# Root of the variance in the first node stage: ACT's square root for two blocks in place of a Newton iteration on DVE

## The chip, the cores and the metric

The kernel runs on one core of a Trainium2 chip. The metric is the device time of one execution in microseconds (us): the median of 3 runs was 4217.27 us before the change (4213.93 to 4219.17).

## What is computed

A graph network of four layers over 50,000 nodes with 160 features and 25,000 edges. Every layer ends with a layer norm. Cut to layer 0:

```python
x = layernorm(x + L0(x, node_vec1, edge_attr_4, edge_attr_8, weights, src, dst))   # and so for L1, L2, L3

def layernorm(x, eps=1e-05):
    m = mean(x, axis=-1); v = var(x, axis=-1)
    return (x - m) / sqrt(v + eps)

# L0, after the edges' messages are summed per node into agg and mapped to ms, conv:
sc    = linear(x) * node_attr
angle = 0.1 * (ms @ W3) * node_attr / sqrt(96)
return cos(angle) * sc + sin(angle) * conv
```

Features are held as 64 scalars and 3 x 32 vector components.

## The kernel before

The kernel goes through the layers one by one, each in two stages. An **edge stage** gathers the rows of source nodes, computes messages and writes sums per node to the tensor `aggregates`. A **node stage** goes over the nodes and writes the layer's output. The node stage works on 100 blocks (NBLK) of 512 nodes: 128 partitions with four nodes each, so a block is a tile of 128 x 640 (`xn`, `an`, both in `arena`), held in a ring of 8 (NRING). Every engine has its own instruction sequence, and the order of work is written out by hand: `steps` calls an engine's function for every block b (some 12 blocks unrolled, the rest in a loop of 8 bodies), and waits on semaphores tie the engines together. "Body b" below is one call of such a function. Engines run at different distances from one another, since each body also handles earlier blocks.

In layer 0 the node stage does this:

- **SP** loads x and aggregates (L470, L459).
- **PE** (`node_products`), body b: transposes block b (L794), then the products of block b-1 with the self weights, eight matmuls (L816) that fill one PSUM bank for nodes 0 to 2, and four (L820, L821) that fill the second. `sc_ready` counts both banks.
- **ACT** (`node_copies`), body b: issues the store of block b-5 (L926), copies the transposed block b out of PSUM to `nT` (L930), normalizes block b-4 by four instructions with `rstd` as scale and `shift` as bias (L950), and in even bodies computes Abs and two sines for the pair of blocks that begins at b+2 (`sines`, L909, L910, L912).
- **POOL** (`node_moves`): in even bodies the gates of a pair from its sines (L596, L597), a copy of gate inputs (L563), and the angles of the next pair, a chain of eight small steps (L578 to L585) that ends with `trig_ready`. In every body it multiplies the aggregates by a gate (L625) and adds them to x (L632), which counts `x_added`.
- **DVE** (`node_vectors`), body b: four multiply-adds that add the gated products to x (L1268; the first two wait for the first bank of products and for `x_added`, the third for the second bank), four `bn_stats` (L1276), four `bn_aggr` (L1287) that leave mean and variance in `mv` and count `mv_ready`. In even bodies the root of the variance of the pair (b-2, b-1) is interleaved with these: `root()` issues the next instruction of a chain of twelve. It adds EPS (L1204), makes a guess from the bits as an int32 operation (L1205), does three Newton steps (L1207, L1208, L1209), which end in `rstd`, and computes `shift` = -mean x rstd (L1210). Each waits for the one before by `root_chain`, and `shift_ready` lets ACT normalize.

Layers 1 to 3 have no such chain: ACT computes `std` by Sqrt per block (L944), DVE the reciprocal and the shift (L1233, L1238). Where ACT's next function isn't in the table that is loaded, the compiler puts an ACT_TABLE_LOAD into the sequence. Before the change layer 0 has none between Silu of its edge stage and Sin, Abs, Copy and Identity of its node stage, and layers 1 to 3 have one each ahead of their first Sqrt.

Of the kernel before, what the change touches and what calls it, by code (L numbers as in the profile page):

```python
# [22 lines left out]
P = 128  # L23
BT = 4
NBLK = 100
# [25 lines left out]
ZN = 3240  # L51
TWO_PI_HI = 6.28125
TWO_PI_LO = float(2 * np.pi - 6.28125)
GUESS = float(0x5f3759df)
ROUND = 12582912.0

r = lambda n: float(1.0 / np.sqrt(float(n)))
# [87 lines left out]
def steps(eng, first, last, steady, body, ring=RING):  # L145

    lo, hi = steady
    for q in range(first, lo):
        body(q, q % ring, q // ring)
    with eng.Fori(0, (hi - lo) // ring) as i:  # L150
        for k in range(ring):
            body(i * ring + (lo + k), k, i + lo // ring)
    for q in range(hi, last):
        body(q, q % ring, q // ring)


def within(q, lo, hi):

    return lo <= q < hi if isinstance(q, int) else True
# [14 lines left out]
def build(nc, nodes, front, back_rows, gate_rows, pairs, eattr, main, small, self_rows, out):  # L174
# [3 lines left out]
    with ctx:  # L178
        def sb(name, shape, dt=f32):
            return ctx.enter_context(nc.sbuf_tensor(name, shape, dt))  # L180

        def sem(name):
            return ctx.enter_context(nc.semaphore(name))
# [54 lines left out]
        stats = sb("stats", [P, 2, BT, 6])  # L238
        mv = sb("mv", [P, NRING, BT, 2])
        std = sb("std", [P, NRING, BT])  # L240
        var = sb("var", [P, 2, BT])
        newton = sb("newton", [P, 3, 2, BT])
        rstd = sb("rstd", [P, NRING, BT])
        shift = sb("shift", [P, NRING, BT])
        gates = sb("gates", [P, NRING, BT, 2])
# [72 lines left out]
        tot_ready, carried, tot_out = sems("tot_ready", 2), sems("carried", 2), sem("tot_out")  # L318


        y_part, count_max = sem("y_part"), sem("count_max")
        TRIG_OPS, ROOT_OPS = 8, 11
        PC2 = TRIG_OPS // 2 * NBLK
        x_in, a_in, stored = sems("x_in", NRING), sems("a_in", NRING), sems("stored", NRING)
        nturned, nturned_out, sc_ready = sem("nturned"), sem("nturned_out"), sem("sc_ready")
# [522 lines left out]
        def _(act):  # L848
# [8 lines left out]
            for l in range(4):  # L857
# [60 lines left out]
                def node_copies(b, k, turn):  # L918
                    if within(b, STORE_LAG[l], NBLK + STORE_LAG[l]):
                        kk, tt = back(k, turn, STORE_LAG[l], NRING)  # L920
                        done = b - STORE_LAG[l]
                        if not isinstance(b, int):
                            done = act.snap(done)
                        act.wait_ge(normed, node_count(l, b - STORE_LAG[l]))
                        alone(act, passed["act"])
                        act.dma_start(orows[bass.ds(done, 1)].rearrange("o p c -> (o p) c"), xn[:, kk]).then_inc(stored[kk], 16)  # L926
                    if within(b, 0, NBLK):
                        act.wait_ge(nturned, node_count(l, b))
                        wait(act, sc_ready, 2 * (b + (l * NBLK - 1)))
                        nc.scalar.activation(nT[:, k % 2, :], two_banks[k % 2][:, 0:5 * P], ACT.Copy).then_inc(nturned_out, 1)  # L930
                        if l == 0 and isinstance(b, int) and b == 0:
                            sines(b, k)
                    if l == 3 and within(b, 0, NBLK):
                        act.wait_ge(gates_ready, b + (2 * NBLK + 1))
                        act.wait_ge(a_in[k], node_slot(l, k, turn) * 16)
                        alone(act, passed["act"])
                        for j in range(BT):
                            row = an3[:, k, j, F:2 * F]
                            last = nc.scalar.activation(row, row, ACT.Copy, scale=gates[:, k, j, 1:2])  # L939
                        last.then_inc(second_gated, 1)  # L940
                    if l and within(b, SQRT_LAG, NBLK + SQRT_LAG):
                        kk, tt = back(k, turn, SQRT_LAG, NRING)
                        act.wait_ge(mv_ready, node_count(l, b - SQRT_LAG))
                        nc.scalar.activation(std[:, kk, :], mv[:, kk, :, 1], ACT.Sqrt, bias=eps[:, :]).then_inc(std_ready, 1)  # L944
                    if within(b, APPLY_LAG[l], NBLK + APPLY_LAG[l]):
                        kk, tt = back(k, turn, APPLY_LAG[l], NRING)
                        act.wait_ge(shift_ready, node_count(l, b - APPLY_LAG[l]))
                        for t in range(BT):
                            row = xn[:, kk, t * F:(t + 1) * F]
                            last = nc.scalar.activation(row, row, ACT.Identity,  # L950
                                                        bias=shift[:, kk, t:t + 1], scale=rstd[:, kk, t:t + 1])
                        last.then_inc(normed, 1)
                    if l == 0 and k % 2 == 0 and within(b, 0, NBLK - 2):
                        sines(b + 2, (k + 2) % NRING)
# [5 lines left out]
        def _(dve):  # L960
# [135 lines left out]
            for l in range(4):  # L1096
# [98 lines left out]
                def node_vectors(b, k, turn):  # L1195
                    k2 = k % 2
                    base = b * 2 + 2 * l * NBLK
                    kk, tt = back(k, turn, 1, NRING)
                    ka = (k - 2) % NRING if k % 2 == 0 else 0
                    stt = nc.vector.scalar_tensor_tensor  # L1200

                    v, (y, a, c) = var[:, :, :], (newton[:, n] for n in range(3))
                    R = rstd[:, ka:ka + 2, :]
                    ops = [lambda: nc.vector.tensor_scalar(v, mv[:, ka:ka + 2, :, 1], EPS, None, ALU.add),  # L1204
                           lambda: nc.vector.tensor_scalar(y.bitcast(i32), v.bitcast(i32), -0.5, GUESS, ALU.mult, ALU.add)]  # L1205
                    for n in range(3):
                        ops += [lambda: stt(out=a, in0=y, scalar=-0.5, in1=v, op0=ALU.mult, op1=ALU.mult),  # L1207
                                lambda: nc.vector.tensor_tensor(c, a, y, ALU.mult),  # L1208
                                lambda to=y if n < 2 else R: stt(out=to, in0=c, scalar=1.5, in1=y, op0=ALU.add, op1=ALU.mult)]  # L1209
                    ops.append(lambda: stt(out=shift[:, ka:ka + 2, :], in0=mv[:, ka:ka + 2, :, 0], scalar=-1.0, in1=R,  # L1210
                                           op0=ALU.mult, op1=ALU.mult))
                    done = [0]
                    rooted = l == 0 and k % 2 == 0 and within(b, 2, NBLK + 1)

                    def root(n=1):
                        for _ in range(n):
                            i = done[0]
                            if not rooted or i > ROOT_OPS:
                                return
                            if i == 0:  # L1220
                                dve.wait_ge(mv_ready, b)
                            else:
                                dve.wait_ge(root_chain, (b - 2) * ROOT_OPS + 2 * i)
                            if i < ROOT_OPS:
                                ops[i]().then_inc(root_chain, 2)
                            else:
                                ops[i]().then_inc(shift_ready, 2)
                            done[0] += 1
# [60 lines left out]
                            last.then_inc(mv_ready, 1)  # L1289
                        root()  # L1290

                steps(dve, 0, NBLK + 1, NODE_STEADY, node_vectors, NRING)

# [36 lines left out]
```

## Time and profile before

| what | value |
|---|---|
| median of 3 runs | 4217.27 us (4213.93 to 4219.17) |
| profiled execution: its own time | 4216.08 us |
| its span, first to last instruction | 4214.4 us |
| busy share of the span | PE 85%, DVE 70%, POOL 61%, ACT 52% |
| node stage of layer 0 | about 700 to 1210 us |
| mean granted TensorE clock, whole span | 0.935 of full speed |

Busy shares of the whole span are averages over eight stages that differ in what limits them. The profile is one execution; the time outside its span is 1.7 us. In its views a line number is one of the kernel before, a name `arena<-bank` says what an instruction writes and reads, "x4" counts merged instructions, and a part in brackets gives the idle time ahead of it and what ended it.

### The profile page before, as it was taken

How to read it: one execution, taken by the hardware profiler on the slowest of the kernel's cores; microseconds unless marked ns; L12 is line 12 of the kernel's file. 1: busy time of each engine (PE TensorE's matmuls, PEld its weight loads, DVE VectorE, ACT ScalarE, POOL GpSimd, SP SyncE). 2: the span in 40 equal slices, each digit the busy share in tenths (PEclk: the TensorE clock that was granted, in tenths of full speed). 3: DMA queues.
4: the chain of work that ended last, by engine and by line, in shares of the span. 5: the costliest groups of instructions: out<-in, count | busy, mean ns of one | idle time of the engine just before them, and what ended most of it. 6: DMA issues, size and time to landing. Idle time of an engine off the chain costs nothing. (4 is left out here: it accounts for less than half of the span.)

```text
span 4214.4 us, 104663 instructions
## 1 busy us (share of the span) xinstructions
PE 3591.9 (85%) x27044; PEld 3337.9 (79%) x27044; DVE 2936.2 (70%) x10747; ACT 2187.2 (52%) x5797; POOL 2567.6 (61%) x3126
## 2 busy tenths in 40 slices
PE   0699997666669999899989999899799999877676
PEld 0599996656569999877779999777699999866566
DVE  0577775888866666488856666688766666588888
ACT  0244443555544444377744444577655555477777
POOL 0377776777757777500057777444456666488887
PEclk9999998777779999999989999999999999988988
DMA  9522223666556555488832222588622222277775
GB/s 380 183 74 62 60 54 99 197 200 201 198 164 178 174 173 171 140 284 299 294 81 62 61 58 52 172 281 280 225 69 74 73 69 62 62 260 259 246 257 193
DMA packets 469538, 682.78 MB, mean 162 GB/s; under 512 B 212838, under 2 KB 285502, under 8 KB 465672
## 3 DMA queue, kind: packets, MB, share of 16 engines
q1 hardware_dynamic: 333546, 389.79, 30.2%
q0 software_dynamic: 75376, 125.21, 10.6%
q10 hardware_dynamic: 60512, 166.57, 10.0%
q8 instruction: 44, 0.72, 0.1%
q14 instruction: 60, 0.49, 0.0%
HBM read 391.37 MB, written 314.78 MB: 168 GB/s over the span
## 5 line engine op out<-in xcount | busy, mean ns | idle before, releaser
L537 POOL DMA_INDIRECT aggregates<-arena,meta x784 | 793.3, 1012 | 445.0 <-issue 240.8
L950 ACT ACTIVATE arena<-arena,shift,rstd 128x160 f32<-128x160 f32 x1600 | 697.2, 507 | 180.2 <-DVE shift L1210 177.7
L717 PE MATMUL bank<-same_all,msg 128*98 (+1 forms) x6272 | 753.4, 274 | 0.0
L528 POOL DMA_INDIRECT xg<-x_after,meta x588 | 575.9, 979 | 272.1 <-issue 251.0
L717 PEld LDWEIGHTS bank<-same_all,msg 128*98 128x98 f32 x6272 | 711.1, 166 | 0.0
L884 ACT ACTIVATE w<-bank 1x162 f32<-1x162 f32 (+1 forms) x784 | 257.2, 328 | 788.1 <-PE bank L750 782.2
L750 PE MATMUL bank<-w,arena 98*128 98x32 f32 (+1 forms) x4704 | 626.3, 270 | 0.0
L816 PEld LDWEIGHTS bank<-sc_cols,nT 128*128 128x128 f32 x2400 | 360.4, 221 | 290.2 <-issue 288.9
L750 PEld LDWEIGHTS bank<-w,arena 98*128 98x128 f32 x4704 | 588.0, 192 | 0.0
L1268 DVE SCALAR_TENSOR_TENSOR arena<-bank,attr,arena 128x160 f32<-128x160 f32 x1600 | 519.9, 378 | 88.3 <-PE bank L816 25.4
L816 PE MATMUL bank<-sc_cols,nT 128*128 128x128 f32 (+1 forms) x2400 | 373.0, 307 | 179.8 <-ACT nT L930 162.9
L1276 DVE BATCH_NORM_STATS2 stats<-arena 128x6 f32<-128x160 f32 x1600 | 456.3, 315 | 55.6 <-DVE arena L1268 14.1
L930 ACT ACTIVATE nT<-bank 128x640 f32<-128x640 f32 x400 | 281.3, 704 | 336.6 <-PE bank L816 161.4
L827 PE MATMUL bank<-sc_cols,nT 128*128 128x128 f32 (+4 forms) x1600 | 331.3, 369 | 131.8 <-DVE arena L1268 124.1
L1155 DVE TENSOR_TENSOR arena<-bank,yv 128x192 f32<-128x192 f32 x294 | 105.2, 358 | 472.2 <-PE bank L765 280.3
L827 PEld LDWEIGHTS bank<-sc_cols,nT 128*128 128x128 f32 x1600 | 288.1, 222 | 174.3 <-issue 153.1
L760 PE MATMUL bank<-weights,xT 128*128 128x128 f32 (+1 forms) x2940 | 405.6, 280 | 4.2 <-DVE msg L1180 4.2
L760 PEld LDWEIGHTS bank<-weights,xT 128*128 128x128 f32 x2940 | 365.1, 194 | 5.2 <-DVE msg L1180 5.1
L794 PE MATMUL bank<-ident,arena 128*128 128x128 f32 x2000 | 324.8, 299 | 47.6 <-DMA arena<-x_after 35.1
L794 PEld LDWEIGHTS bank<-ident,arena 128*128 128x128 f32 x2000 | 269.3, 167 | 49.9 <-issue 49.7
L1127 DVE COPY arena<-bank 98x512 f32<-98x512 f32 x392 | 268.6, 685 | 48.2 <-PE bank L717 26.3
L872 ACT ACTIVATE arena<-bank 98x512 f32<-98x512 f32 x392 | 234.2, 597 | 123.1 <-PE bank L717 113.1
(142 smaller groups left out, 6832.0 us busy)
## 6 DMA issues: line engine op xcount, KB each, us to landing
arena<-aggregates SPq DMA_DIRECT2D x300, 324.0 KB, 4.3
x_after<-arena ACTq DMA_DIRECT2D x300, 320.0 KB, 3.6
arena<-x_after SPq DMA_DIRECT2D x300, 320.0 KB, 3.8
aggregates<-zeros SPq DMA_DIRECT2D x100, 640.0 KB
same_all<-aggregates SPq DMA_DIRECT2D x100, 640.0 KB, 5.2
aggregates<-same_all ACTq DMA_DIRECT2D x4, 8100.0 KB, 71.7
arena<-nodes SPq DMA_DIRECT2D x100, 320.0 KB, 3.1
out<-arena ACTq DMA_DIRECT2D x100, 320.0 KB, 3.9
```

What stands on the lines that cost most here:

```text
L528: gp.indirect_dma_start(xg[:, k % XGR, 4 + t * F:4 + (t + 1) * F], None, xtab[l], at).then_inc(gathered[k], 16)
L537: gp.indirect_dma_start(agg if l < 3 else agg3, at, tot[:, kk % TRING, t, 0:aw[l]], None, bounds_check=NP - 1, oob_is_err=False).then_inc( ...
L717: last = nc.tensor.matmul(bank[5 + t][0:MR, c * P:(c + 1) * P], msg[:, k2, t, c, :], same_all[:, bass.ds(here[t], P)], start=True, stop=True)
L750: last = nc.tensor.matmul(to, aggT[:, t, (d + 1) * P:(d + 2) * P], of, start=True, stop=True)
L760: last = nc.tensor.matmul(bank[3 + g][:, a:e], xT[:, k2, c * P:(c + 1) * P], w1[l][:, g * W1C + a:g * W1C + e], start=True, stop=True)
L794: last = nc.tensor.transpose(to[:, c * P:(c + 1) * P], xn[:, k, c * CH:(c + 1) * CH], ident[:, :])
L816: last = mm(A[:, o:e], turned_x[c], sc[l][:, o:e], start=fresh, stop=fresh or c == 3)
L827: return mm(two(bank[4 + j][:, 0:2 * F], F)[:, :, lo:hi], turned_x[c], W[:, :, at:at + hi - lo], **flags)
L930: nc.scalar.activation(nT[:, k % 2, :], two_banks[k % 2][:, 0:5 * P], ACT.Copy).then_inc(nturned_out, 1)
L950: last = nc.scalar.activation(row, row, ACT.Identity, bias=shift[:, kk, t:t + 1], scale=rstd[:, kk, t:t + 1])
L1268: last = stt(out=row, in0=ob[:, o + g * F:o + (g + 1) * F], scalar=gate, in1=row, op0=ALU.mult, op1=ALU.add)
L1276: last = nc.vector.bn_stats(stats[:, k2, j, :], xn[:, k, j * F:(j + 1) * F])
```

## The change

In layer 0, ACT takes the square root of variance + eps for both blocks of a pair at once, in even bodies from 2 on, after the copy to `nT` and ahead of the normalizations. It waits for `mv_ready` = b, that is, for the statistics of block b-1, and counts `first_std`. DVE's chain of twelve becomes two instructions, a reciprocal and the shift, and moves from the even body to the odd one after it, so DVE's function runs for one more body. APPLY_LAG and STORE_LAG stay as they are.

```diff
--- before.py
+++ after.py
@@ -51,7 +51,6 @@
 ZN = 3240
 TWO_PI_HI = 6.28125
 TWO_PI_LO = float(2 * np.pi - 6.28125)
-GUESS = float(0x5f3759df)
 ROUND = 12582912.0
 
 r = lambda n: float(1.0 / np.sqrt(float(n)))
@@ -238,8 +237,6 @@
         stats = sb("stats", [P, 2, BT, 6])
         mv = sb("mv", [P, NRING, BT, 2])
         std = sb("std", [P, NRING, BT])
-        var = sb("var", [P, 2, BT])
-        newton = sb("newton", [P, 3, 2, BT])
         rstd = sb("rstd", [P, NRING, BT])
         shift = sb("shift", [P, NRING, BT])
         gates = sb("gates", [P, NRING, BT, 2])
@@ -318,8 +315,9 @@
         tot_ready, carried, tot_out = sems("tot_ready", 2), sems("carried", 2), sem("tot_out")
 
 
+        first_std = sem("first_std")
         y_part, count_max = sem("y_part"), sem("count_max")
-        TRIG_OPS, ROOT_OPS = 8, 11
+        TRIG_OPS, ROOT_OPS = 8, 1
         PC2 = TRIG_OPS // 2 * NBLK
         x_in, a_in, stored = sems("x_in", NRING), sems("a_in", NRING), sems("stored", NRING)
         nturned, nturned_out, sc_ready = sem("nturned"), sem("nturned_out"), sem("sc_ready")
@@ -942,6 +940,10 @@
                         kk, tt = back(k, turn, SQRT_LAG, NRING)
                         act.wait_ge(mv_ready, node_count(l, b - SQRT_LAG))
                         nc.scalar.activation(std[:, kk, :], mv[:, kk, :, 1], ACT.Sqrt, bias=eps[:, :]).then_inc(std_ready, 1)
+                    if l == 0 and k % 2 == 0 and within(b, 2, NBLK + 1):
+                        ka = (k - 2) % NRING
+                        act.wait_ge(mv_ready, b)
+                        nc.scalar.activation(std[:, ka:ka + 2, :], mv[:, ka:ka + 2, :, 1], ACT.Sqrt, bias=eps[:, :]).then_inc(first_std, 2)
                     if within(b, APPLY_LAG[l], NBLK + APPLY_LAG[l]):
                         kk, tt = back(k, turn, APPLY_LAG[l], NRING)
                         act.wait_ge(shift_ready, node_count(l, b - APPLY_LAG[l]))
@@ -1196,21 +1198,15 @@
                     k2 = k % 2
                     base = b * 2 + 2 * l * NBLK
                     kk, tt = back(k, turn, 1, NRING)
-                    ka = (k - 2) % NRING if k % 2 == 0 else 0
+                    ka = (k - 3) % NRING if k % 2 else 0
                     stt = nc.vector.scalar_tensor_tensor
 
-                    v, (y, a, c) = var[:, :, :], (newton[:, n] for n in range(3))
                     R = rstd[:, ka:ka + 2, :]
-                    ops = [lambda: nc.vector.tensor_scalar(v, mv[:, ka:ka + 2, :, 1], EPS, None, ALU.add),
-                           lambda: nc.vector.tensor_scalar(y.bitcast(i32), v.bitcast(i32), -0.5, GUESS, ALU.mult, ALU.add)]
-                    for n in range(3):
-                        ops += [lambda: stt(out=a, in0=y, scalar=-0.5, in1=v, op0=ALU.mult, op1=ALU.mult),
-                                lambda: nc.vector.tensor_tensor(c, a, y, ALU.mult),
-                                lambda to=y if n < 2 else R: stt(out=to, in0=c, scalar=1.5, in1=y, op0=ALU.add, op1=ALU.mult)]
-                    ops.append(lambda: stt(out=shift[:, ka:ka + 2, :], in0=mv[:, ka:ka + 2, :, 0], scalar=-1.0, in1=R,
-                                           op0=ALU.mult, op1=ALU.mult))
+                    ops = [lambda: nc.vector.reciprocal(R, std[:, ka:ka + 2, :]),
+                           lambda: stt(out=shift[:, ka:ka + 2, :], in0=mv[:, ka:ka + 2, :, 0], scalar=-1.0, in1=R,
+                                       op0=ALU.mult, op1=ALU.mult)]
                     done = [0]
-                    rooted = l == 0 and k % 2 == 0 and within(b, 2, NBLK + 1)
+                    rooted = l == 0 and k % 2 and within(b, 3, NBLK + 2)
 
                     def root(n=1):
                         for _ in range(n):
@@ -1218,9 +1214,9 @@
                             if not rooted or i > ROOT_OPS:
                                 return
                             if i == 0:
-                                dve.wait_ge(mv_ready, b)
+                                dve.wait_ge(first_std, b - 1)
                             else:
-                                dve.wait_ge(root_chain, (b - 2) * ROOT_OPS + 2 * i)
+                                dve.wait_ge(root_chain, b - 1)
                             if i < ROOT_OPS:
                                 ops[i]().then_inc(root_chain, 2)
                             else:
@@ -1289,7 +1285,7 @@
                             last.then_inc(mv_ready, 1)
                         root()
 
-                steps(dve, 0, NBLK + 1, NODE_STEADY, node_vectors, NRING)
+                steps(dve, 0, NBLK + (1 if l else 2), NODE_STEADY, node_vectors, NRING)
```

How ACT's sequence moves, in the loop of layer 0's node stage. Before, from the wait for the transposes of an even body to that of the next (L930 copy, L950 normalization, L909 to L912 Abs and sines, L926 store):

```order
L166 REGISTER_ALU [waits nturned]
L930 ACTIVATE nT<-bank 128x640 [waits sc_ready]
L950 ACTIVATE arena<-arena,shift,rstd 128x160 [waits shift_ready]
L950 ACTIVATE arena<-arena,shift,rstd 128x160 x3
L906 REGISTER_ALU
L909 ACTIVATE trig<-trig 128x2x4 [waits gates_ready,trig_ready]
L910 ACTIVATE waves<-trig 128x2x4
L912 ACTIVATE waves<-trig,half_pi 128x2x4 [waits abs_ready]
L926 ISA [waits normed]
L926 DMA x_after<-arena 128x640
L166 REGISTER_ALU [waits nturned]
L930 ACTIVATE nT<-bank 128x640 [waits sc_ready]
```

Now, the same place (lines of the changed kernel: L928 copy, L946 root, L952 normalization, L907 to L910 Abs and sines):

```order
L165 REGISTER_ALU [waits nturned]
L928 ACTIVATE nT<-bank 128x640 [waits sc_ready]
L946 ACT_TABLE_LOAD [waits mv_ready]
L946 ACTIVATE std<-mv,eps 128x8
L952 ACTIVATE arena<-arena,shift,rstd 128x160 [waits shift_ready]
L952 ACTIVATE arena<-arena,shift,rstd 128x160 x3
L904 REGISTER_ALU
L907 ACTIVATE trig<-trig 128x2x4 [waits gates_ready,trig_ready]
L908 ACT_TABLE_LOAD
L908 ACTIVATE waves<-trig 128x2x4
L910 ACTIVATE waves<-trig,half_pi 128x2x4 [waits abs_ready]
L924 ISA [waits normed]
```

Two table loads and the root are new; the first load holds the wait for `mv_ready`. Such a group stands in each even body. The very last root, in body 100, has no load in front of it, since no sines come between it and the one before.

DVE's even body before, from its first multiply-add (L1268) on (the rest of the chain follows between the `bn_stats` and `bn_aggr`):

```order
L1268 SCALAR_TENSOR_TENSOR arena<-bank,gates,arena 128x160 [waits sc_ready]
L1204 TENSOR_SCALAR var<-mv 128x8 [waits mv_ready]
L1268 SCALAR_TENSOR_TENSOR arena<-bank,gates,arena 128x160
L1223 ISA
L1205 TENSOR_SCALAR newton<-var 128x8 [waits root_chain]
L1260 REGISTER_ALU
L1268 SCALAR_TENSOR_TENSOR arena<-bank,gates,arena 128x160 [waits sc_ready]
L1223 REGISTER_ALU
L1207 SCALAR_TENSOR_TENSOR newton<-newton,var 128x8 [waits root_chain]
L1268 SCALAR_TENSOR_TENSOR arena<-bank,gates,arena 128x160
L1223 REGISTER_ALU
L1208 TENSOR_TENSOR newton<-newton 128x8 [waits root_chain]
```

Now its odd body, from its first multiply-add (L1264) on; L1205 is the reciprocal, L1206 the shift:

```order
L1264 SCALAR_TENSOR_TENSOR arena<-bank,gates,arena 128x160 [waits sc_ready]
L1205 RECIPROCAL rstd<-std 128x8 [waits first_std]
L1264 SCALAR_TENSOR_TENSOR arena<-bank,gates,arena 128x160
L1206 SCALAR_TENSOR_TENSOR shift<-mv,rstd 128x8 [waits root_chain]
L1256 REGISTER_ALU
L1264 SCALAR_TENSOR_TENSOR arena<-bank,gates,arena 128x160 [waits sc_ready]
L1264 SCALAR_TENSOR_TENSOR arena<-bank,gates,arena 128x160
L1272 BN_STATS stats<-arena 128x6 [waits y_stt]
L1272 BN_STATS stats<-arena 128x6 x3
L1283 BN_AGGR mv<-stats 128x2 [waits stats_ready]
L1283 BN_AGGR mv<-stats 128x2 x3
```

The chain is gone from between the instructions, and the even body holds statistics alone.

## Rows read from the trace of the kernel before

**Rows 1.** Windows: start:end, length, busy of PE, PEld, DVE, ACT, POOL, clock, DMA

```profile
720.00:1200.00 480.00, 305.65 (x1622) 282.30 (x1622) 409.60 (x1749) 253.76 (x622) 358.79 (x708) 0.72 0.58 191
```

**Rows 2.** Waits, 720 to 1200 us: who for whom, total us, times, longest

```profile
ACT arena L950 <- DVE shift L1210: 175.5, 49, 7.4
...
POOL arena L632 <- POOL arena L625: 19.9, 96, 0.5
...
POOL arena L625 <- POOL trig L585: 18.5, 47, 0.4
```

**Rows 3.** Timeline of POOL, one pair of blocks: start, length, what

```profile
902.18 1.26 POOL L625 TENSOR_TENSOR arena<-arena,gates 128x640 f32<-128x640 f32 x1 [0.40 <-POOL trig L585]
...
907.88 0.20 POOL L596 TENSOR_TENSOR gates<-waves,attr 128x8 f32<-128x8 f32 x1
...
912.04 1.26 POOL L625 TENSOR_TENSOR arena<-arena,gates 128x640 f32<-128x640 f32 x1 [0.40 <-POOL trig L585]
```

**Rows 4.** Timeline of ACT, second sines of body 2 and of body 96

```profile
713.99 0.30 ACT L912 ACTIVATE waves<-trig,half_pi 128x8 f32<-128x8 f32 x1
...
1180.77 0.30 ACT L912 ACTIVATE waves<-trig,half_pi 128x8 f32<-128x8 f32 x1
```

**Rows 5.** Groups of instructions, 720 to 1200 us: busy us, mean ns

```profile
L1205 DVE TENSOR_SCALAR newton<-var 128x8 int32<-128x8 int32 x48 | 67.1, 1398 | 0.0
...
L1204 DVE TENSOR_SCALAR var<-mv 128x8 f32<-128x8 f32 x48 | 32.9, 685 | 0.0
```

**Rows 6.** POOL's line L632: shortest, median and longest of 100, ns

```profile
L632 POOL TENSOR_TENSOR arena<-arena x100: 1419/1426/1436, 705.4 to 1190.0; 128x640 f32<-128x640 f32 x100
```

**Rows 7.** Groups, whole span: DVE's reciprocal of 128x8 in layer 2

```profile
L1193 DVE RECIPROCAL inv_count<-inv_count 128x8 f32<-128x8 f32 x50 | 10.1, 203 | 5.4
```

**Rows 8.** Timeline of ACT, node stage of layer 1: a table load

```profile
1794.41 0.70 ACT L930 ACTIVATE nT<-bank 128x640 f32<-128x640 f32 x1 [3.84 <-PE bank L794]
1795.13 1.28 ACT L944 ACT_TABLE_LOAD   x1
1796.43 0.30 ACT L944 ACTIVATE std<-mv,eps 128x4 f32<-128x4 f32 x1
```

**Rows 9.** Timeline of ACT, layer 0: normalizations, Abs, sines and the next copy

```profile
901.36 1.75 ACT L950 ACTIVATE arena<-arena,shift,rstd 128x160 f32<-128x160 f32 x4 [3.51 <-DVE shift L1210]
903.02 0.20 ACT L909 ACTIVATE trig<-trig 128x8 f32<-128x8 f32 x1
903.12 0.19 ACT L910 ACTIVATE waves<-trig 128x8 f32<-128x8 f32 x1
903.31 0.30 ACT L912 ACTIVATE waves<-trig,half_pi 128x8 f32<-128x8 f32 x1
...
904.07 0.70 ACT L930 ACTIVATE nT<-bank 128x640 f32<-128x640 f32 x1 [0.46 <-issue]
```

**Rows 10.** Timeline of PE: products of a block, in three places

```profile
905.01 1.56 PE L816 MATMUL bank<-sc_cols,nT 128*128 128x128 f32 x8 [4.12 <-ACT nT L930]
...
908.75 1.18 PE L816 MATMUL bank<-sc_cols,nT 128*128 128x128 f32 x8 [0.20 <-DVE arena L1268]
...
1195.48 2.00 PE L816 MATMUL bank<-sc_cols,nT 128*128 128x128 f32 x8 [7.92 <-ACT nT L930]
...
1197.85 0.53 PE L821 MATMUL bank<-sc_cols,nT 128*128 128x64 f32 x2
```

**Rows 11.** Timeline of DVE: an odd body

```profile
911.48 1.26 DVE L1268 SCALAR_TENSOR_TENSOR arena<-bank,gates,arena 128x160 f32<-128x160 f32 x4 [0.18 <-issue]
912.89 1.01 DVE L1276 BATCH_NORM_STATS2 stats<-arena 128x6 f32<-128x160 f32 x4 [0.15 <-DVE arena L1268]
914.05 0.38 DVE L1287 BATCH_NORM_AGGREGATE mv<-stats 128x2 f32<-128x6 f32 x4
```

**Rows 12.** Timeline of ACT: last normalizations of the stage

```profile
1207.82 1.75 ACT L950 ACTIVATE arena<-arena,shift,rstd 128x160 f32<-128x160 f32 x4 [0.55 <-ACT arena L950]
```

**Rows 13.** Timeline of POOL and DVE: a small operation beside a large one

```profile
1185.74 1.25 POOL L625 TENSOR_TENSOR arena<-arena,gates 128x640 f32<-128x640 f32 x1 [0.20 <-POOL gates L597]
1185.81 1.21 DVE L1208 TENSOR_TENSOR newton<-newton 128x8 f32<-128x8 f32 x1
```

## Prediction

> **What bounds the kernel now.** The change acts in the node stage of layer 0 only, so I first look at that stretch by itself. Over 480 us of it DVE is busy for 409.6, POOL for 358.8, PE for 305.7 and ACT for 253.8 [rows 1]. By these shares DVE is the engine to relieve. The waits of the same stretch say otherwise [rows 2]: POOL waits for its own preceding instructions, never for ACT or DVE, while ACT stands 175.5 us waiting for DVE's shift. POOL's timeline shows the same [rows 3]. From one gate multiplication (L625) of an even block, at 902.18, to the next, at 912.04, are 9.86 us, in which POOL runs two multiplications, two additions, the two gate products at 907.88 and a chain of small steps for the angles, one behind the other. Its idle time is the chain's own latency. So a period of two blocks is POOL's 9.86 us. The sines of two neighbouring periods give the same: L912 ends at 714.29 in the first full round and at 1181.07 in the last, 47 periods later [rows 4], or 9.93 us each. DVE's small operations are stretched by POOL (below), which raises its busy time without its being the bound.
>
> **What is removed.** Per pair DVE loses eleven small operations; the shift, the twelfth of the chain, moves from the even body to the odd one. The two dearest are the int32 guess (L1205, 1398 ns on average) and the add of EPS (L1204, 685 ns) [rows 5]. That relieves DVE by over 2 us per pair, yet POOL doesn't wait for DVE, and its addition L632 lasts 1419 to 1436 ns all through the stage [rows 6], so it isn't stretched by DVE either. I book the removal at nothing while POOL's 9.86 us cover it. A reciprocal of 128x8, added, is 203 ns in another layer [rows 7].
>
> **What is added on ACT.** One root of 128x8 per pair, near 0.3 us like the 128x4 one, and, as the listing in the section on the change shows, two table loads per pair: one before the root, one before the sine that follows. The load before the root carries the wait for `mv_ready`, so it begins only when DVE has finished the pair's statistics. A load takes 1.28 us, and with its edges 1.30: the copy before it ends at 1795.11, the root after it begins at 1796.43 [rows 8]. In work alone this fits: ACT's 253.8 us of 480 are 5.2 per period of 9.86, and 2 x 1.30 + 0.3 more make 8.1.
>
> **The wait is what costs.** ACT used to run two blocks ahead of DVE. Now, in even body b, it stands behind the statistics of block b-1; behind that wait are queued four normalizations (L950), the sines, and the copy of block b+1 (L930) that PE needs for the products that DVE needs for block b+1, whose statistics the next root awaits. That is a closed loop, once per pair, and I add it up from the end of the sines:
>
> - end of L912 at 903.61 to the copy at 904.07, with the store's issue in front: 0.46; the copy itself 0.70 [rows 9]
> - its end at 904.77 to PE's first product at 905.01: 0.24; the eight products that release DVE (A): 1.56 there, 2.00 after a longer idle time at 1195.48 [rows 10]; I take 1.7, nearer to the first, since PE will stand idle some 3 to 5 us ahead of them, raised a little since its busy share falls and a granted clock under the present mean of 0.72 [rows 1], nearer the lower level (1.2 GHz, 0.5), is to be expected
> - DVE's body for block b+1: 2.95 from 911.48 to 914.43 [rows 11], plus 0.1 to start, plus 0.3 since its third operation must wait for the second half of the products, which end 0.90 after the first [rows 10], plus 0.05 for the two small operations: 3.4
> - DVE to ACT: 0.05, an estimate; load 1.30; root 0.20 until the next may start; four normalizations 1.75; Abs 0.10 beyond them; load 1.30; two sines 0.49 [rows 8, 9]
>
> The sum is 0.46 + 0.70 + 0.24 + 1.70 + 3.40 + 0.05 + 1.30 + 0.20 + 1.75 + 0.10 + 1.30 + 0.49 = 11.69 us. It exceeds 9.93, so this loop becomes the bound, and POOL will wait for sines. 47 periods x (11.69 - 9.93) = 82.7 us. At the start of the stage two loads and a root in front of the second sines cost about 2.0 (an estimate). At the end it gives something back: before, from the last sines at 1181.07 to the last normalization's end at 1209.57 [rows 4, 12] are 28.5 us, since the eleven chained steps come last; after, it is 6.55 (the loop up to the wait) + 1.30 + 0.20 + 1.75 (root and block 96), 6.55 again, then 0.20 and four normalizations, 1.75 and three more with their 0.55 of gap (8.65) = 25.2: 3.3 less. In sum 82.7 + 2.0 - 3.3 = +81.4. The profiled execution took 4216.1 us (span 4214.4), 1.2 under the median of 4217.3; on the median that gives 4298.7, rounded **4299 us**. Nothing absorbs it later: the next edge stage's gathers wait for the last stores of this one.
>
> Bounds of the terms: A between 1.2 (the row at 908.75, 1.18, where PE had hardly paused) and 2.0, so a period of 11.2 to 12.0, +58 to +96; the estimates for the edges may be off by 0.15 per period, 7 us in all. The forecast's own range is 4268 to 4320.
>
> The Trainium skill ("ScalarE: Activation LUTs", What ACT_TABLE_LOAD costs) has a switch of table sets at 1283 ns of load plus about 1380 ns of drain, 2.66 us in all. The load's 1283 ns agree with the row, the drain does not show: the load begins 0.02 us after the copy and is followed by the root 0.02 us after its end [rows 8]. The rule would make of each loop 1.38 x 2 more; it is the third rival below.
>
> **Rivals.**
>
> *Not slower: the loads are hidden.* The price is the two loads, the place ACT's body b. Without the loads the loop is 11.69 - 2.60 = 9.09 us and POOL's 9.93 stay the bound. It would take the load before the root being done during the wait (ACT should stand idle for about 2.5 us there) and A at 1.2: 11.69 - 1.30 - 0.5 = 9.89, under the deciding point of 9.93, so 4217. Against it: the listing puts the wait on the load. Chance 0.05, plus 0.02 that DVE's relief brings a gain that I don't see (the tail alone gives 3.3, under 0.2%).
>
> *Half hidden.* The first load hidden, A as forecast: 10.39, +0.46 x 47 - 1.3 = +20, so 4238. Chance 0.06.
>
> *Drain.* Each switch costs 1.38 us beyond the load because ACT has to run empty before it: the period is 11.69 + 2.76 = 14.45, 47 x 4.52 = 212, with the loads at both ends +215, so about 4432. In the only such rows ACT was empty or nearly so before the load, though the copy in front of it was in flight until 0.02 us before; in the loop the first load follows a wait, too. Chance 0.04.
>
> *A new stall on DVE.* At 1185.81 a 128x8 product of two SBUF operands took 1.21 us instead of 0.17, just while POOL's L625 ran from 1185.74 [rows 13]. The new shift operation has two SBUF operands as well. It stands some 0.7 us into DVE's odd body, at 1.40 + A + 0.1 + 0.7 after the sines' end; POOL's L625 begins about 4.16 after its gate products [rows 3], which themselves wait for those sines, so at 4.26. With A = 2.0 the shift comes at 4.2: by a hair it is in front; a slip of 0.1 puts it behind, and DVE's third operation comes 0.95 later (1.25 less the 0.3 for which it waits anyway). Period 12.94, 47 x 3.01 - 1.3 = +140, so 4357. The Trainium skill ("GPSIMD Engine Reference", Specifications) has GpSimd's SBUF interfaces shared with VectorE, in contention with instructions of two SBUF inputs; the row at 1185.81 agrees. Chance 0.12.
>
> That the change wouldn't do what it says is excluded by the listing.
>
> **How the numbers follow.** Forecast 0.68 (4268 to 4320), new stall 0.12, half hidden 0.06, hidden 0.05, drain 0.04, DVE gain 0.02, others 0.03. The range has to hold forecast and stall: 4262 to 4362, with some room on both sides, and leaves out the other 0.20. A measurement of this kernel tells about 0.2% (8 us) from no change. Faster by more: 0.02. Within: 0.05. Slower: 0.93.
>
> **What the profile after would show.** Some 100 table loads of 1283 ns in this stage, 50 at the root and 47 or 48 at the sine; the idle time before the root's load given to DVE's `mv`, and longer than any other on ACT; L625 to L625 on POOL 11.7 us apart with a new wait of its gate products for ACT's `waves`, near 1.8 us each; DVE and PE with idle time before each odd block, ended by the copy and the products; DVE's small operations gone, and no 1.4 us instruction left; stages after it unchanged in length. The prediction is wrong if POOL's period stays near 9.9, if an ACT gap of over 1 us stands beside each load, or if ACT's wait for `mv` isn't there at all.

## The result, and the profile after

The changed kernel took 4273.88 us, the median of 4 runs (4270.72 to 4280.35), against 4215.60 us for the kernel before in 4 (4213.63 to 4219.17): a ratio of 1.0139, 95% interval 1.0122 to 1.0157. That is 58 us slower. The forecast was 4299, 81 us slower; the measured time lies in the stated range of 4262 to 4362 and in the forecast's own range of 4268 to 4320.

The profiled execution took 4273.99 us (span 4272.3). In its node stage of layer 0, the window that answers to [rows 1] (its columns are the same):

```profile
720.00:1240.00 520.00, 289.12 (x1572) 279.50 (x1571) 255.44 (x1206) 365.64 (x736) 349.19 (x702) 0.73 0.50 173
```

DVE has fallen from 85% to 49% busy, and the stage takes longer. ACT has become the busiest, yet at 70%: no engine is full. That is the sign of a loop of waits. The waits of the stage (who for whom, total us, times, longest) name its members, and answer to [rows 2]:

```profile
PE bank L814 <- ACT nT L928: 230.9, 46, 5.9
DVE arena L1264 <- PE bank L814: 164.9, 46, 4.0
ACT L946 <- DVE mv L1283: 118.8, 46, 5.3
POOL gates L594 <- ACT waves L910: 59.3, 44, 1.9
```

PE waits for ACT's copy, DVE for PE's products, ACT's table load for DVE's statistics, each some 46 times, that is once per pair. POOL, the bound before, now waits 59.3 us for ACT's sines.

One round on ACT, from sines to sines, answers to [rows 8, 9]:

```profile
1010.19 0.28 ACT L910 ACTIVATE waves<-trig,half_pi 128x8 f32<-128x8 f32 x1
1010.39 0.68 ACT L928 ACTIVATE nT<-bank 128x640 f32<-128x640 f32 x1
...
1016.69 1.28 ACT L946 ACT_TABLE_LOAD   x1 [2.49 <-DVE mv L1283]
1017.98 0.30 ACT L946 ACTIVATE std<-mv,eps 128x8 f32<-128x8 f32 x1
1018.19 1.74 ACT L952 ACTIVATE arena<-arena,shift,rstd 128x160 f32<-128x160 f32 x4
1019.84 0.19 ACT L907 ACTIVATE trig<-trig 128x8 f32<-128x8 f32 x1
1020.04 1.28 ACT L908 ACT_TABLE_LOAD   x1
1020.34 0.34 ACTq L924 DMA_DIRECT2D x_after<-arena  x1
1021.34 0.21 ACT L908 ACTIVATE waves<-trig 128x8 f32<-128x8 f32 x1
1021.45 0.28 ACT L910 ACTIVATE waves<-trig,half_pi 128x8 f32<-128x8 f32 x1
```

PE's and DVE's part of the same round, from two timelines, answers to [rows 10, 11]:

```profile
1011.31 1.99 PE L814 MATMUL bank<-sc_cols,nT 128*128 128x128 f32 x8 [5.22 <-ACT nT L928]
```

```profile
1013.34 0.38 DVE L1264 SCALAR_TENSOR_TENSOR arena<-bank,gates,arena 128x160 f32<-128x160 f32 x1 [3.66 <-PE bank L814]
1013.64 0.19 DVE L1205 RECIPROCAL rstd<-std 128x8 f32<-128x8 f32 x1
...
1013.99 0.16 DVE L1206 SCALAR_TENSOR_TENSOR shift<-mv,rstd 128x8 f32<-128x8 f32 x1
...
1016.23 0.38 DVE L1283 BATCH_NORM_AGGREGATE mv<-stats 128x2 f32<-128x6 f32 x4 [0.15 <-DVE stats L1272]
```

The whole loop can be walked without a gap: sines' end 1010.47, copy to 1011.07, products 1011.31 to 1013.30, DVE's odd body 1013.34 to 1016.61, load from 1016.69, sines' end 1021.73. The round is 11.26 us. In the line of ACT's second sine (shortest, median, longest ns; first and last start) stands the length of the stage, before and after:

```profile
L912 ACT ACTIVATE waves<-trig,half_pi x50: 300/301/303, 699.4 to 1180.8; 128x8 f32<-128x8 f32 x50
```

```profile
L910 ACT ACTIVATE waves<-trig,half_pi x50: 284/285/301, 699.9 to 1246.7; 128x8 f32<-128x8 f32 x50
```

From first to last sines are 481.4 us before and 546.8 after. Below, this distance is called the **sine span**.

Not all of these 65.4 us reach the end. From the last sines' end, 1247.01, to the last normalization's end are 24.8 us in place of 28.5 [rows 4, 12]:

```profile
1270.07 1.75 ACT L952 ACTIVATE arena<-arena,shift,rstd 128x160 f32<-128x160 f32 x4 [0.50 <-ACT arena L952]
```

At the start of layer 1's edge stage another 3.1 come back: in the windows up to its fourth copy, before and after, the same 86 matmuls (in the third field) are done in 17.8 and 14.7 us, at a granted clock (the field after POOL's) of 0.62 and 0.82.

```profile
1219.60:1237.40 17.80, 16.22 (x86) 15.30 (x86) 7.15 (x19) 4.00 (x11) 9.19 (x10) 0.62 0.58 167
```

```profile
1282.40:1297.10 14.70, 12.61 (x86) 11.89 (x86) 6.68 (x19) 3.99 (x11) 9.17 (x10) 0.82 0.69 201
```

So 65.4, plus 0.5 for a later start, less 3.7, puts the changed kernel 62.2 us behind at the end of the stage. Layer 1's first copy comes 62.8 us later than before, and from its fourth to the end of its edge stage every copy 59.7 later. From there to the end the lag still moves by one or two us, both ways: 57.8 in layer 2's edge stage, 56.7 in layer 3's, 57.9 at the end, which is the difference of the two spans.

One thing looks as if it should give 1.3 us back: layer 0 leaves the table of the root in place, so layer 1 needs no load ahead of its first root, and two loads are left at that line in place of three. It gives 0.2. The copy in front of that root comes at 1853.03 in place of 1794.41 [rows 8], 58.6 later, and the root at 1854.88 in place of 1796.43, 58.5 later, since without the load ACT stands waiting for DVE's statistics:

```profile
1853.03 0.70 ACT L928 ACTIVATE nT<-bank 128x640 f32<-128x640 f32 x1 [3.14 <-PE bank L792]
1854.88 0.30 ACT L942 ACTIVATE std<-mv,eps 128x4 f32<-128x4 f32 x1 [1.14 <-DVE mv L1283]
```

### The profile page after: what moved, and what is told of

Its sections match the earlier page's. It is cut to its first block, busy times and chain, and to the rows that moved or that the text cites. A ratio compares the mean times of both kernels' runs of the same rounds, so it can differ in the third digit from the quotient of the medians.

```text
span 4272.3 us, 103386 instructions
## 1 busy us (share of the span) xinstructions
PE 3579.7 (84%) x27044; PEld 3338.2 (78%) x27044; DVE 2792.6 (65%) x10247; ACT 2322.2 (54%) x5943; POOL 2568.7 (60%) x3126
## 4 chain that ended last, share of the span: by engine, by line
PE 59%; DVE 17%; issue 8%; ACT 5%; POOL 3%; DMA 2%; another core or an unknown queue 1%; ACTq 1%; SPq 1%; DVEq 1%; POOLq 1%
PE bank L715 16%; PE bank L748 12%; DVE arena L1264 8%; PE bank L758 8%; DVE stats L1272 4%; PE bank L766 3%; PE bank L705 3%; PE bank L763 3%; PE bank L722 3%; ACT arena L952 3%; PE bank L814 2%; PE bank L740 2%; PE bank L811 2%; DVE shift L1234 2%; DVE mv L1283 2%
## 5 line engine op out<-in xcount | busy, mean ns | idle before, releaser
L952 ACT ACTIVATE arena<-arena,shift,rstd 128x160 f32<-128x160 f32 x1600 | 696.3, 507 | 3.0 <-ACT arena L952 3.0
L1264 DVE SCALAR_TENSOR_TENSOR arena<-bank,attr,arena 128x160 f32<-128x160 f32 x1600 | 518.8, 378 | 82.9 <-PE bank L814 25.5
L1272 DVE BATCH_NORM_STATS2 stats<-arena 128x6 f32<-128x160 f32 x1600 | 445.0, 313 | 58.9 <-DVE arena L1264 9.4
L928 ACT ACTIVATE nT<-bank 128x640 f32<-128x640 f32 x400 | 280.6, 702 | 316.5 <-PE bank L814 171.0
L1264 DVE SCALAR_TENSOR_TENSOR arena<-bank,gates,arena 128x160 f32<-128x160 f32 x400 | 132.5, 374 | 272.4 <-PE bank L814 172.4
```

Source lines behind the costliest of these rows:

```text
L952: last = nc.scalar.activation(row, row, ACT.Identity, bias=shift[:, kk, t:t + 1], scale=rstd[:, kk, t:t + 1])
L1264: last = stt(out=row, in0=ob[:, o + g * F:o + (g + 1) * F], scalar=gate, in1=row, op0=ALU.mult, op1=ALU.add)
L1272: last = nc.vector.bn_stats(stats[:, k2, j, :], xn[:, k, j * F:(j + 1) * F])
```

## The experiments

Ten kernels were run. They fell on three chips: on the first (runs e1, e2, e3, e6) the kernel before took 4215.7 us, on the others 5008.6 (e9, e4, e8, e5) and 5042.4 (e7, e10), since the edge stages are slower there (the first sines begin at 894 to 906 us in place of some 700). So a time is compared only with the kernel before on its own chip, and the sine span tells what the stage did; ACT's and POOL's instructions in it last as long on all three. No profile of the kernel before was taken on the other two chips, so that its sine span is 481.4 us there too is assumed and not shown.

### e1_no_loads: the wait without the loads

```diff
-nc.scalar.activation(std[:, ka:ka + 2, :], mv[:, ka:ka + 2, :, 1], ACT.Sqrt, bias=eps[:, :]).then_inc(first_std, 2)
+nc.scalar.activation(std[:, ka:ka + 2, :], mv[:, ka:ka + 2, :, 1], ACT.Identity, bias=eps[:, :]).then_inc(first_std, 2)
```

> The changed kernel with Identity in place of Sqrt in layer 0 (so layer 0 is normalized by the reciprocal of variance + eps instead of that of its root), which needs no table loads; the wait for mv_ready and all the order stay. Theory L (a closed loop ACT - PE - DVE through the wait, 11.26 us long, of which 2 x 1.30 are loads): the loop falls to 8.66 us, under POOL's 9.86 to 9.93, so the period from sines to sines goes back to 9.9 and the time to 4211 to 4217. Theory W (the wait alone costs it, wherever ACT stands behind DVE's statistics): the period stays near 11 and the time above 4255. Theory D (DVE's relief would show once nothing else is in the way): under 4205.

Measured: 4212.73 us in 10 runs, ratio 0.9992 (0.9982 to 1.0002). Sine span and largest wait on ACT:

```profile
L910 ACT ACTIVATE waves<-trig,half_pi x50: 300/300/302, 701.5 to 1182.3; 128x8 f32<-128x8 f32 x50
```

```profile
ACT std L946 <- DVE mv L1283: 153.0, 46, 7.3
```

480.8 us, as before the change. ACT waits even longer for DVE's statistics (153 us), and that costs nothing: the wait alone is harmless. The time lies in the 4211 to 4217 that I expected if the loop was the cause. DVE's relief doesn't show in the period either.

### e2_odd_root: the loads without that wait

```diff
-                    if l == 0 and k % 2 == 0 and within(b, 2, NBLK + 1):
-                        ka = (k - 2) % NRING
-                        act.wait_ge(mv_ready, b)
+                    if l == 0 and k % 2 and within(b, 3, NBLK + 2):
+                        ka = (k - 3) % NRING
+                        act.wait_ge(mv_ready, b - 1)
```

> The changed kernel with the root moved on ACT from the even body b (pair b-2, b-1) to the odd body b+1, behind its copy, so the same statistics are awaited one block later; the two table loads per pair and the correct root stay. Theory L: the copy for block b+1 no longer stands behind the wait, the longest loop left is some 7.2 us (shift, normalizations, load, sines, copy, products), POOL is the bound again: period 9.9, time 4210 to 4217, with some 96 table loads left in the stage. Theory T (the loads cost the time as work of ACT, 2.6 us per pair wherever they stand): the period stays 11.0 or more, time above 4260.

Measured: 4209.13 us in 10 runs, ratio 0.9984 (0.9974 to 0.9993), so 65 us faster than the changed kernel (4273.88), with as much work on ACT. It is also 6.6 us faster than the kernel before, just outside the 4210 to 4217 that I expected; the sine span below doesn't hold that gain, and where it lies wasn't looked into.

```profile
L910 ACT ACTIVATE waves<-trig,half_pi x50: 284/285/302, 703.7 to 1185.4; 128x8 f32<-128x8 f32 x50
```

The line of the root, with its waits:

```profile
L946 ACT ACT_TABLE_LOAD  x48: 1283/1283/1283, 719.2 to 1186.3; - x48
its engine sat idle before it (us, times) until:
  DVE mv L1283: 0.8, 1
```

The sine span is 481.7 us with 48 loads at the root alone. The wait for `mv`, 118.8 us before, is 0.8. So the loads as work of ACT cost nothing, either. It takes both, the loads and the place behind the wait, to lengthen the period.

### e3_short_chain: the removal on DVE alone

```diff
-                    ops = [lambda: nc.vector.tensor_scalar(v, mv[:, ka:ka + 2, :, 1], EPS, None, ALU.add),
-                           lambda: nc.vector.tensor_scalar(y.bitcast(i32), v.bitcast(i32), -0.5, GUESS, ALU.mult, ALU.add)]
...
+                    ops = [lambda: nc.vector.tensor_scalar(R, mv[:, ka:ka + 2, :, 1], EPS, None, ALU.add)]
```

> The kernel before with the chain on DVE cut from twelve instructions to two (variance + eps goes straight into rstd, no guess and no Newton steps, so layer 0 is scaled wrongly by design of the test); nothing is added on ACT. It is the removal on DVE alone. POOL-bound theory: period 9.86 to 9.93 as before, time 4209 to 4216 (only the tail of some 2.7 us may go). Theory D (DVE was the bound or next to it): the period falls by up to 1 us and the time under 4190.

Measured: 4204.57 us in 10 runs, ratio 0.9972 (0.9963 to 0.9982): 11 us faster, where I had 4209 to 4216.

```profile
L912 ACT ACTIVATE waves<-trig,half_pi x50: 300/301/302, 698.5 to 1178.9; 128x8 f32<-128x8 f32 x50
```

The sine span, 480.4, is 1.0 us under that of before, so the period did not move. The gain is in the tail: its last normalization begins at 1199.02 and ends at 1200.77, 21.6 us after the last sines' end, in place of 28.5.

```profile
1199.02 1.75 ACT L950 ACTIVATE arena<-arena,shift,rstd 128x160 f32<-128x160 f32 x4 [0.50 <-ACT arena L950]
```

Of these 6.9 us, 2.7 are the chain behind the last statistics, as expected: 3.30 us from their end to the shift's end before, 0.57 here. The other 4.2 come ahead of it. In the last rounds POOL has no angles left to compute and its multiplications follow one another, and DVE's small operations stall beside them, as in [rows 13]; before, with six such stalls of 0.8 to 1.4 us in one body, DVE fell behind there. Of the 10.7 us between the two profiled executions (spans 4214.4 and 4203.7) 6.9 lie there, 1.0 in the sine span and 0.9 before the first sines; the other 1.9 I can't place.

### e9_load_first: one load taken out of the loop

```diff
+                        nc.scalar.activation(early[:, :], eps[:, :], ACT.Sqrt)
                         act.wait_ge(mv_ready, b)
```

> The changed kernel with one tiny Sqrt (128x1, of eps, result unused) on ACT ahead of the wait for mv_ready, so that the table load before the root runs during that wait; all loads and the true root stay. Theory L: one load, 1.30 us, leaves the loop of 11.26: 9.96 us, which stands within 0.05 of POOL's 9.93, so the period is 9.93 to 10.05 and the time 4210 to 4218. Theory T (loads cost what they take on ACT, wherever they stand): period 11.3 or a little more, since work is added, time above 4268.

Measured: 5013.29 us in 10 runs against 5008.58, ratio 1.0001 (0.9980 to 1.0023). The sine span:

```profile
L911 ACT ACTIVATE waves<-trig,half_pi x50: 283/285/302, 893.7 to 1377.1; 128x8 f32<-128x8 f32 x50
```

483.4 us, 2.0 more than the kernel before had on the first chip (the time that I expected, 4210 to 4218, was one of that chip; here only the ratio can be compared). The 47 rounds have a mean of 9.95 us, and 31 of them lie between 9.97 and 10.03, on the loop's 11.26 - 1.30 = 9.96. ACT now executes one instruction more than in the changed kernel and the loss is gone: a load costs its length if it stands behind the wait, and nothing ahead of it. The timeline shows the load inside the former idle time:

```profile
1004.32 1.28 ACT L946 ACT_TABLE_LOAD   x1
1005.62 0.20 ACT L946 ACTIVATE early<-eps 128x1 f32<-128x1 f32 x1
1006.55 0.30 ACT L948 ACTIVATE std<-mv,eps 128x8 f32<-128x8 f32 x1 [0.73 <-DVE mv L1285]
```

### e4_two_copies, e8_three_copies, e5_four_copies: other work in the loads' place

The edit of e1, and two, three or four of these behind the wait:

```diff
+                        nc.scalar.activation(spare[:, 0], weights[:, 0:640], ACT.Copy)
```

> e1_no_loads with two copies of 128x640 into a spare tile on ACT behind the wait for mv_ready, some 0.62 us each, so the loop is 8.66 + 1.24 = 9.9 us instead of the 1.30 x 2 of the loads (layer 0 is normalized without the root, as in e1). Theory L: at the threshold of 9.93: period 9.93 to 10.0, time 4210 to 4220.

> As e4_two_copies with three copies: loop 8.66 + 1.86 = 10.5. Theory L: period 10.5, time about 4240. If ACT's work below some fixed reserve were free and then dear at once, or if the loads had a cost of their own, the period would not rise by the copies' own length.

> As e4_two_copies with four copies: loop 8.66 + 2.48 = 11.1. Theory L: period 11.1 (0.6 more than with three), time about 4267, near the changed kernel's 4274 with no table load in the stage at all.

Measured, one execution each: 5029.11, 5048.09 and 5101.03 us, on a chip where the kernel before ranged from 4980 to 5025 in 13. The sine spans, in this order, tell it more finely:

```profile
L911 ACT ACTIVATE waves<-trig,half_pi x50: 300/301/303, 899.0 to 1397.3; 128x8 f32<-128x8 f32 x50
```

```profile
L911 ACT ACTIVATE waves<-trig,half_pi x50: 300/301/302, 900.9 to 1433.4; 128x8 f32<-128x8 f32 x50
```

```profile
L911 ACT ACTIVATE waves<-trig,half_pi x50: 300/300/302, 905.9 to 1469.0; 128x8 f32<-128x8 f32 x50
```

They are 498.3, 532.5 and 563.1 us. The usual round is 10.37, 11.00 and 11.63 us: each copy adds 0.63, which is just its own pitch on ACT. So the loads have no cost beyond their length, and ordinary copies in their place lengthen the stage in the same way. But all three rounds are 0.5 us longer than I expected, and e4 was to stand at the threshold and stands over it. The loop without copies is 11.63 - 4 x 0.63 = 9.11 us, not 8.66. The 0.45 between them is the store's issue. In the changed kernel it runs beside the second table load (1020.34, within the load from 1020.04), and the copy begins 0.08 us before the sines' end; so it does in e2 and e9, which have that load too. Without a load there, in e1, e4, e8 and e5 as in the kernel before, the issue stands between sines and copy, which begins 0.40 behind their end in most rounds and 0.46 in every fourth or fifth, as in [rows 9]; in e5:

```profile
1003.37 0.30 ACT L911 ACTIVATE waves<-trig,half_pi 128x8 f32<-128x8 f32 x1
1003.59 0.34 ACTq L925 DMA_DIRECT2D x_after<-arena  x1
1004.13 0.70 ACT L929 ACTIVATE nT<-bank 128x640 f32<-128x640 f32 x1 [0.46 <-issue]
```

From e5's usual round to the changed kernel's the copy moves forward by 0.40 + 0.08 = 0.48, and the first load begins 0.05 us later behind DVE's statistics (0.08) than e5's first copy does (0.03). 9.11 + 2 x 1.30 - 0.48 + 0.05 = 11.28, where the walk above gave 11.26.

### e6_add_on_dve and e10_lead_four: using DVE's room

e2's root, and the addition moved from POOL to DVE:

```diff
-                    if l == 2:
+                    if l in (0, 2):
                         return
                     gp.wait_ge(gated, gated_count(b))
...
+                    if l == 0:
+                        dve.wait_ge(gated, b + 1)
+                        dve.wait_ge(nturned, b + 1)
+                        alone(dve, passed["dve"])
+                        x = xn[:, k].rearrange("p (t c) -> p t c", t=BT)
+                        nc.vector.tensor_tensor(x, x, an[:, k, :, 2:AW], ALU.add).then_inc(x_added, 1)
```

> e2_odd_root, and in layer 0 the addition of the gated aggregates to x (1.43 us per block on POOL) is moved to DVE, at the start of its body. POOL then has 9.86 - 2 x 1.63 = 6.6 us of work per pair, DVE 5.5 + 2 x 0.7 = 6.9 plus stalls beside POOL's multiplication, ACT 8.1. If POOL was the bound and the loop through the wait is gone, the period falls to 8.1 to 9.2 and the time to 4130 to 4190. If another loop near 9.9 binds (ACT's order), it stays 4210 to 4217; if DVE's stalls beside POOL (up to 1.2 us each) take over, the period is 9.5 to 10.5.

Measured: 4185.22 us in 4 runs, ratio 0.9929 (0.9913 to 0.9946): 30 us faster than the kernel before. The sine span is 460.0; rounds wander between 8.8 and 11.1 us with a mean of 9.52. The time lies in the expected 4130 to 4190, but the period misses its 8.1 to 9.2 and stands where I had put stalls of DVE beside POOL. Its trace named a new wait instead:

```profile
POOL trig L576 <- DMA arena<-aggregates: 61.1, 32, 3.2
```

e10 is e6 with `A_LEAD = 4` in place of 2, so the aggregates are requested two blocks sooner.

> e6_add_on_dve with aggregates loaded four blocks ahead of x instead of two (A_LEAD 4), since its trace shows POOL waiting 61 us for that load in the stage and a period that wanders between 8.8 and 11.1 us. If the load binds, the period falls to 8.8 to 9.2 and the ratio to the kernel before from 0.993 to 0.985 to 0.990; if ACT's order binds, the period stays 9.5 and the ratio 0.993.

Measured: 4999.02 us in 6 runs against 5042.35, ratio 0.9917 (0.9890 to 0.9944).

```profile
L910 ACT ACTIVATE waves<-trig,half_pi x50: 283/285/303, 902.3 to 1330.0; 128x8 f32<-128x8 f32 x50
```

The sine span is 427.7 and nearly every round 8.77 us, and no wait of POOL for a DMA is left in the stage, so waiting for that load is what had held e6 back. The ratio lies above the 0.985 to 0.990 that I gave, though its interval reaches down to 0.9890. It wasn't run on the chip on which e6 ran, so how far it beats e6 in time stays open; in the stage it is 32 us.

### e7_before_add: the same move without the change

The same edit as e6's, applied to the kernel before, with its Newton chain.

> The kernel before (Newton chain on DVE) with the addition of the gated aggregates to x moved from POOL to DVE, as in e6_add_on_dve. If DVE's room was what kept POOL's relief from paying, the move costs here: DVE has 8.4 us busy per pair already, so 9.8 or more with the additions, plus stalls beside POOL; period 10.0 to 11.5, ratio to the kernel before 1.001 to 1.018. If POOL's relief alone makes the gain of e6_add_on_dve and the root's place doesn't matter, the ratio is near e6's 0.993.

Measured: 5155.86 us in 4 runs against 5042.35, ratio 1.0247 (1.0202 to 1.0293).

```profile
L912 ACT ACTIVATE waves<-trig,half_pi x50: 300/301/303, 899.1 to 1473.6; 128x8 f32<-128x8 f32 x50
```

The sine span is 574.5, worse than foreseen: most rounds are 11.2 to 11.4 us and every fourth 14.5. DVE is busy for 425.6 of 520 us of the stage, more than any other engine, ACT waits 245.7 us for its shift and POOL 207.4 us for ACT's sines; that DVE alone is the bound is a reading of this and was not tested. Its chain stalls in this version too (1.01 us for a small product beside POOL's multiplication):

```profile
1106.33 2.47 POOL L625 TENSOR_TENSOR arena<-arena,gates 128x640 f32<-128x640 f32 x2 [0.40 <-POOL trig L585]
...
1106.60 1.01 DVE L1207 SCALAR_TENSOR_TENSOR newton<-newton,var 128x8 f32<-128x8 f32 x1
```

So the room that the change makes on DVE is real: the same move costs time with the chain there and gains with it gone. It pays only once POOL's work is moved into it. The move with the root left in its even body wasn't run; that the odd place is needed for it rests on e2. What makes every fourth round 14.5 wasn't looked into.

## Why the prediction was right, point by point

- **POOL is the bound before, not DVE.** That it isn't DVE is shown by e3 (chain cut to two instructions, sine span unchanged) and e1. That it is POOL rests on its own rows [rows 2, 3] and on e6, where taking two additions per round from it brought e2's mean round from 9.94 to 9.52 us.
- **What is removed costs nothing while POOL covers it.** Right for the period. At the end of the stage my sum had 3.3 us less for the net of chain and new root, and 3.7 were measured; what cutting the chain alone gives there, 6.9 in e3, I had at 2.7.
- **A closed loop through the wait becomes the bound.** Shown by e1, e2 and e9 from three sides; e1 and e2 each undo one of its two conditions.
- **The size of the loop, 11.69 us, was 0.43 too long,** and this is the step that was mis-sized: with the mean round of the trace it is 47 x (11.28 - 9.93) = 63.4 us in place of 82.7, which is 19 of the 25 us by which the forecast was off; another 4.3 lie in later stages (below). By terms: from the sines' end to the copy I had 0.46 for the store's issue, and it is -0.08, since the issue runs beside the second load: -0.54. This term I took from a row without a load in front of it, and did not ask what the load would do to it. The first eight products (A) take 1.99 in place of 1.70: +0.29. DVE's body from A's end is 3.31 for 3.40, the sines 0.39 for 0.49, the copy 0.68 for 0.70, the way to the load 0.08 for 0.05, the Abs and the second load together 0.01 more: -0.17 in all. The two large errors have opposite signs, so the period came out better than its parts, and that is luck. The measured time lies 6 us above the lower end of the forecast's own range.
- **The clock.** A took 1.99 us in nearly every round, behind some 5.2 us of idle time on PE. That is its length at the lower level (1.2 GHz), as the granted clock (the field after POOL's) of 0.50 shows; the next eight of the same round (second line) took 1.03 us at 1.00 there, and between 1.03 and 1.86 in the others, as the clock rose earlier or later.

```profile
1011.31:1013.30 1.99, 1.99 (x9) 1.99 (x10) 0.00 (x0) 1.40 (x4) 1.08 (x5) 0.50 0.39 85
1014.80:1015.83 1.03, 1.03 (x11) 1.03 (x10) 0.88 (x5) 0.00 (x0) 0.93 (x1) 1.00 0.59 234
```

I had gone nearer to the row with 4.1 us of idle time; the row at 1195.48 was the right one. I also expected the mean granted clock of the stage to fall; it went from 0.72 to 0.73.
- **Nothing absorbs it later.** Wrong by 4.3 us in sum (62.2 at the end of the stage, 57.9 at the end). 3.1 come back at the start of layer 1's edge stage, where PE's clock rose sooner; the rest is the balance of shifts of one or two us in later stages, of which the table load that layer 1 no longer needs makes 0.2. Why the clock rose sooner is not known, and no run was made for it or for the later shifts.
- **The drain.** The Trainium skill's 1.38 us beside each load ("ScalarE: Activation LUTs", What ACT_TABLE_LOAD costs) shows nowhere in this case: the second load of the round begins within 0.02 us of the Abs' end, the first stands behind the wait and begins 0.08 us after DVE's statistics, the next instruction follows either by 0.02 us or less, and e5's arithmetic closes to 0.02 with 1.30 per load.
- **The new stall on DVE** did not come: the shift lasts 0.16 us at 1013.99, and POOL's multiplication begins in that round only at 1014.90, 0.75 us after the shift's end. I had them within 0.1 of each other; the copy's earlier start made most of that room.
- **Half hidden** was set at 0.46 us per round over POOL. e9 puts the loop with one load hidden at 9.96, at the threshold; the rival's price carried the same 0.43 error.
- **The signs.** There are 49 loads at the root (the last root has none, as the listing said) and 48 at the sine, in place of 50 and 47 or 48. POOL waits for the sines 1.35 us a round (59.3 / 44), for which I had 1.8, and the stages behind did not keep their length (above).

## What to carry to other kernels

An engine's busy share, and its work per period, don't tell what an addition costs: ask what stands behind the new wait in the same sequence, and whether the awaited result itself hangs on it. If it does, the loop's length counts, and each instruction in it costs its full duration once the loop is longer than the bound of before; moving it one step in the order, or touching its table ahead of the wait, took the whole loss away here (e2, e9). And relief of an engine that isn't the bound is room and not time, until work of the one that is can be moved into it.

## What was not expected of the hardware

- ACT's queue issues a store while the engine loads a table: the issue of 0.34 us lies within the load of 1.28, and the 0.39 to 0.46 us between sines and copy that most rounds have without that load are gone in every round with it: the copy begins 0.08 before the sines' end.
- The kernel before takes 4216 us on one chip and 5009 and 5042 us on two others. POOL's multiplication in this stage has a median of 1256 ns on all three (after, e9, e10), and ACT's second sine one of 285.
